# Three edits to the order of loads and turns in a graph network kernel: one load stage for attention tiles, an earlier transpose of f3, and a longer prefetch ahead of the expert weights

## The chip, the cores and the metric

The kernel runs on one core of a Trainium2 chip. The metric is the time of one execution on the device in microseconds (us), as a median over runs. The names of the engines: PE is TensorE (PEld its weight load), DVE is VectorE, ACT is ScalarE, POOL is GpSimd, SP is SyncE, which here only issues DMA transfers.

## The reference

The reference computes two layers of a graph network over 6250 nodes with 256 features and 100,000 edges, all in float32. Each layer has a message part over the edges, an attention part and a part with experts. Cut to the parts that the edits touch:

```python
# layer 0, attention: linear attention over all nodes, for each row n
q, k = elu(q) + 1, elu(k) + 1
kv = sum_n k[n] v[n]^T                      # per head
z  = 1 / (q . sum_n k[n] + 1e-6)
h  = x_norm + (q @ kv * z) @ w_out + b_out   # x_norm: layer norm of x
out = x + h * (1 + w_norm2 * rsqrt(mean(h * h) + 1e-6))

# layer 1: messages gathered over 100,000 edges, linear attention, sum into x3
f3 = layer_norm(x3)
# layer 1, experts: the router sees the mean of f3 and picks 2 of 8 experts for all rows
g  = softmax over the two picked router values
y  = sum_k g[k] * (gelu(f3 @ W1[k] + b1[k]) @ W2[k] + b2[k])
out = x3 + layer_norm(f3 + y) * gamma + beta
```

## The kernel before

The program is a sequence of phases. Inside a phase every engine has its own instruction stream, written out by the helper `timeline`: a plan gives each stage (a small function of a tile number i) the step at which it starts and a lag, and in each step an engine emits the stages that fall due in it, in the order of the plans. The streams of the engines share no clock. A stage waits on counting semaphores for what it needs (`Steps` for results, `Landing` for transfers), and every stream runs strictly in its own order. So a lag says where in the queue of its engine a stage stands, not when it runs.

Phase **g1** (about 60 to 980 us) is layer 0. POOL gathers rows of the normed input for 702 tiles of 128 edges, one indirect transfer per tile (line 891), in step k for tile k. PE multiplies each pair of gathered tiles with a one-hot matrix (`sums`, line 1285, ten steps after), and DVE adds the product into a ring (line 1098). Woven into that are the attention and the projection of the layer's first matrix (lines 1424 and 969). The attention runs over 50 tiles of 125 rows, one each seven steps (`ATT`), with four buffers (`AR = 4`). For tile i, SP loads `qt` (128 partitions, line 831), `xa` and `x0` (125 partitions each, lines 837 and 841). PE computes the denominators from `qt` eight steps after the tile's first step (line 1354); DVE adds the bias to `xa`, forms h (line 1174) and at the end adds `x0` to give "y" (line 1186, 29 or 30 steps after). Before the change `load_qt` and `load_xa` stand three steps ahead of the tile's first step and wait for "qz" and "h" of tile i-4; `load_x0` stands three steps after it and waits for "y" of tile i-4.

Phase **g2** (about 1680 to 2698 us) is layer 1's message part: 782 gathers (line 2516), two in each step; `sums` (line 2163) five steps after; the DVE add into the ring (line 2646) two steps after that. The PE stage `product(i)` (lines 2805 and 2810) makes the rows of x3 for tile i in step P9[i]+4; DVE's `x3_of(i)` follows in step P9[i]+5 (lines 2709 and 2711, then the row statistics). From step F3[i], which is 12 or more steps after P9[i]: `f3_of(i)` on DVE writes the normed tile (line 1489) in step F3[i], `turned(i)` on PE transposes it (line 2817) in F3[i]+3, `copy(i)` on ACT copies the result out of PSUM and sums it into `fsum` (line 2556) in F3[i]+4, and SP stores f3 (line 2503) in F3[i]+1 and the transposed tile (line 2507) in F3[i]+6. In a step, PE emits `sums` first, then the turns, then the product. `product(49)` is PE's last product; after it only turns are left.

Phase **p11** (from about 2699 us) is the expert part. DVE takes the mean of `fsum`, works out the router on one partition and writes `chosen`; SP reads the two expert numbers from it and loads the weights. Then 25 blocks of 250 rows run through a loop: `layer_up` (32 matmuls, line 2930), gelu on ACT (line 2968), `layer_down` (32 matmuls, line 2947), layer norm on DVE and POOL. PE runs `layer_up(0)`, then two small bias products (line 2939), then `layer_down(0)`, `layer_up(1)` and so on. The first `layer_up` waits for half k of `w1` at the matmuls that use it. SP's stream at the head of the phase: wait for all stores of g2, columns(0) (line 2874, f3 transposed, 128 partitions), rows(0) (lines 2878 and 2880, f3 and x3, 125 partitions), wait for `chosen`, w1 in two halves, b1 in two, columns(1), w2 and b2 in two halves each, gamma, beta, rows(1).

Of the kernel before, what the change touches and what calls it, by code (L numbers as in the profile page):

```python
# [31 lines left out]
N, D, E = 6250, 256, 100000  # L32
P = 128
TN = 125
BN = 2 * TN
NB = N // BN
DC = D // P
# [99 lines left out]
def gps_kernel(nc, A, out):  # L137
# [48 lines left out]
    def spread(dram):  # L186

        return dram.rearrange("(p t) f -> p t f", t=2 * NB)
# [4 lines left out]
    with top:  # L193
# [20 lines left out]
        s_w2 = sem("gin_w2")  # L214
# [410 lines left out]
        with Phase("g1") as ph:  # L625
# [109 lines left out]
            qt_in, xa_in, x0_in = (ph.landing(n, AR) for n in ("qt", "xa", "x0"))  # L735
# [29 lines left out]
            MIX = [QKV[-1] + 27]  # L765
# [33 lines left out]
            with nc.Block() as block:  # L799
                @block.sync  # L800
                def _(e):
# [25 lines left out]
                    def load_qt(i):  # L827
                        if i < 2:
                            q_out.wait(e, i, (NB - 1 - i) // 2)
                        zs.wait(e, i - AR, "qz")  # L830
                        qt_in.start(e.dma_start(qt[:, i % AR, :, :],
                                                q_d[i // 2].rearrange("p (c t n) -> p c t n", c=DC, t=2)
                                                [:, :, i % 2, :]), i % AR)

                    def load_xa(i):
                        hsum.wait(e, i - AR, "h")
                        xa_in.start(e.dma_start(xa[:, i % AR, :], spread(xn_d[0:N, :])[:, i, :]), i % AR)

                    def load_x0(i):
                        fin.wait(e, i - AR, "y")  # L840
                        x0_in.start(e.dma_start(x0[:, i % AR, :], spread(A["x"])[:, i, :]), i % AR)
# [31 lines left out]
                    def load_edges(i):  # L873
# [3 lines left out]
                             (QKV, [(load_xn, 0), (store_q, 23)]), (ATT, [(store_att, 33), (load_x0, 3), (load_xa, -3), (load_qt, -3)]),  # L877
# [115 lines left out]
                def _(e):  # L993
# [171 lines left out]
                    def add_xb(i):  # L1165
                        xa_in.wait(e, i % AR, i // AR)
                        hsum.done(e.tensor_tensor(xa[:, i % AR, :], xa[:, i % AR, :], bout[:, :], ALU.add), "xb")
# [13 lines left out]
                    def finish(i):  # L1181
                        gate.wait(e, i, "g")
                        fin.done(e.tensor_tensor(hh[:, i % AR, :], hh[:, i % AR, :], gw[:, :], ALU.mult), "gh")
                        fin.wait(e, i, "gh")
                        x0_in.wait(e, i % AR, i // AR)
                        fin.done(e.tensor_tensor(hh[:, i % AR, :], hh[:, i % AR, :], x0[:, i % AR, :], ALU.add), "y")
# [66 lines left out]
                def _(e):  # L1253
# [92 lines left out]
                    def denominators(i):  # L1346
                        qt_in.wait(e, i % AR, i // AR)
                        moved.wait(e, i - 1, "den")
                        if i <= ALONE:
                            hsum.wait(e, i - 1, "h")  # L1350
                        if i == 0:
                            mixed.wait(e, 0, "mix")
                        for c in range(DC):
                            mm = e.matmul(ps[:, 3, c * TN:(c + 1) * TN], ksd[:, c, :], qt[:, i % AR, c, :],
                                          start=True, stop=True)
                        dens.done(mm, "den")
# [978 lines left out]
        with Phase("g2") as ph:  # L2335
# [121 lines left out]
            with nc.Block() as block:  # L2457
                @block.sync
                def _(e):
# [45 lines left out]
                    def store_f3T(i):  # L2505
# [3 lines left out]
                             (P9, [(load, 0), (store_x3, 6)]), (F3, [(store_f3, 1), (store_f3T, 6)]))  # L2509
# [13 lines left out]
                def _(e):  # L2523
# [50 lines left out]
                    def do_silu(i):  # L2574
# [6 lines left out]
                             (KV, [(square, 5), (roots, 8)]), (PAIRS, [(deviations, 9)]), (F3, [(copy, 4)]))  # L2581
# [150 lines left out]
                def _(e):  # L2732
# [80 lines left out]
                    def turned(i):  # L2813
                        ln.norm.wait(e, i, "f")
                        copied.wait(e, i - 1, "c1")
                        for c in range(DC):
# [4 lines left out]
                             (KV, [(products, 11), (project, 3)]), (MIX, [(mix_wo, 1), (mix_wq, 3)]), (F3, [(turned, 3)]),  # L2821
# [3 lines left out]
        with Phase("p11") as ph:  # L2825
# [10 lines left out]
            s_in, s_b1, s_w2, s_sc, s_v, s_e, s_pe, s_sel = (  # L2836
                ph.sem(n) for n in ("in", "b1", "w2", "sc", "v", "e", "pe", "sel"))
            s_w1 = [ph.sem(f"w1_{k}") for k in range(2)]
# [26 lines left out]
            with nc.Block() as block:  # L2865
                @block.sync
                def _(e):
# [4 lines left out]
                    def load_columns(i, u, h):  # L2872
                        up.wait(e, i - 2, BANKS[-1])
                        c_in.start(e.dma_start(f3T[:, u, :, :], f3T_d[ds(i * 2, 2), :, :].rearrange("t p n -> p t n")), u)
# [10 lines left out]
                    load_columns(0, 0, 0)  # L2885
                    load_rows(0, 0, 0)
                    e.wait_ge(s_sel, 1)
                    x = [e.value_load(chosen[0:1, k:k + 1], min_val=0, max_val=NE1 - 1) for k in range(2)]  # L2888
                    for k in range(2):
                        e.dma_start(w1[:, k, :, :], A["L1_ffn_W1"][ds(x[k], 1), :, :]  # L2890
                                    .rearrange("e (c p) n -> p (e c) n", p=P)).then_inc(s_w1[k], 16)
# [3 lines left out]
                    load_columns(1, 1, 0)  # L2895
# [4 lines left out]
                    for to, src in ((gamma[:, :], A["L1_ffn_gamma"]), (beta[:, :], A["L1_ffn_beta"])):  # L2900
                        e.dma_start(to, src.partition_broadcast(TN)).then_inc(s_in, 16)
                    load_rows(1, 1, 0)
# [8 lines left out]
                def _(e):  # L2911
# [9 lines left out]
                    def layer_up(i, u, h):  # L2921
                        c_in.wait(e, u, h)
                        for q in range(FC):
                            act.wait(e, i - 1, BANKS[q])
                            for m in range(2):
                                k, f = divmod(2 * q + m, FC)
                                if isinstance(i, int) and i == 0 and f == 0:
                                    e.wait_ge(s_w1[k], 16)
# [161 lines left out]
```

## Time and profile before

| what | value |
|---|---|
| median of 3 runs | 3097.06 us (3095.69 to 3098.36) |
| the profiled execution | 3098.36 us, span of its trace 3096.8 us |
| PE busy | 2645.7 us, 85% of the span |
| DVE, ACT, POOL busy | 1716.6, 1447.5, 1817.0 us |
| granted clock of PE, mean | 0.945 of full speed |
| DMA | 464.78 MB, 150 GB/s over the span |

The span runs from the first to the last instruction of the trace. Busy shares are averages over phases with different limits, so they are read phase by phase. Times in the rows are microseconds from the start of the span. A row of a timeline has the start, the duration, the engine, the line of the kernel, the operation and its tensors (written tensor, then what it reads); "x8" means that many instructions in a row, and a bracket tells how long the engine sat idle before it and what ended that.

### The profile page before, as it was taken

To read this page: it belongs to the slowest core of one execution; us is meant where nothing else is said; L and a number is where in the kernel's file an instruction comes from. 1 tells how busy PE (TensorE), PEld (TensorE's weight loads), DVE (VectorE), ACT (ScalarE), POOL (GpSimd) and SP (SyncE) were. 2 spreads that over 40 slices of the span, in tenths; PEclk is the share of its full clock that TensorE was granted. 3 is DMA by queue.
4 is the path that set the end of the run, shared out by engine and by line. 5 is a ranking of instruction groups with operands and counts; after the bars stand their busy time and mean duration, and the time that the engine had idled before them with its cause. 6 is when DMAs were issued, how large, how long until landed. Compare 5 with 4: busy or idle time off the path is not lost. (4 is left out here: it accounts for less than half of the span.)

```text
span 3096.8 us, 54298 instructions
## 1 busy us (share of the span) xinstructions
PE 2645.7 (85%) x14909; PEld 2211.0 (71%) x14909; DVE 1716.6 (55%) x5340; ACT 1447.5 (47%) x4046; POOL 1817.0 (59%) x1962
## 2 busy tenths in 40 slices
PE   1999998999987997799932999999888888699998
PEld 1777777888886886688832676666677777578876
DVE  7733335787775667333355566566566767633333
ACT  4022222553322553233345988888566766422221
POOL 5777777777774355343376777777777777400000
PEclk9999999999998998899965999999899999899999
DMA  7364446777764674333367444444456665532221
GB/s 226 112 192 141 140 139 187 230 217 229 234 216 124 217 237 152 106 92 94 93 185 237 114 125 116 124 118 125 118 173 185 175 167 158 153 92 70 66 67 55
DMA packets 291701, 464.78 MB, mean 150 GB/s; under 512 B 91221, under 2 KB 224276, under 8 KB 290074
## 3 DMA queue, kind: packets, MB, share of 16 engines
q1 hardware_dynamic: 207804, 232.37, 25.4%
q0 software_dynamic: 81216, 221.98, 24.3%
q10 hardware_dynamic: 2402, 7.19, 0.7%
q8 instruction: 115, 1.88, 0.3%
q14 instruction: 164, 1.34, 0.1%
HBM read 349.16 MB, written 112.23 MB: 149 GB/s over the span
## 5 line engine op out<-in xcount | busy, mean ns | idle before, releaser
L2516 POOL DMA_INDIRECT g_got<-xm_d,idx x782 | 763.6, 977 | 252.9 <-issue 223.3
L891 POOL DMA_INDIRECT g_got<-xn_d,idx x702 | 682.0, 972 | 232.6 <-issue 212.4
L2163 PEld LDWEIGHTS ps<-g_hotw,g_got 128*128 128x128 f32 x3128 | 405.7, 197 | 207.9 <-DMA g_got<-xm_d,idx 107.2
L2163 PE MATMUL ps<-g_hotw,g_got 128*128 128x128 f32 (+11 forms) x3128 | 434.3, 288 | 128.8 <-DMA g_got<-xm_d,idx 70.9
L1285 PEld LDWEIGHTS ps<-g_hot,g_got 128*128 128x128 f32 x2808 | 354.5, 195 | 91.6 <-DMA g_got<-xn_d,idx 57.6
L1285 PE MATMUL ps<-g_hot,g_got 128*128 128x120 f32 (+4 forms) x2808 | 372.3, 280 | 44.5 <-DMA g_got<-xn_d,idx 41.7
L2565 ACT ACTIVATE g_hotw<-g_hot,g_wr 128x16 f32<-128x16 f32 (+8 forms) x1308 | 302.3, 308 | 125.7 <-DVE g_hot L598 125.0
L1485 POOL TENSOR_TENSOR p_ln_rs<-p_ln_pre,neg_half 125x2 f32<-125x2 f32 x50 | 35.2, 703 | 486.9 <-DVE p_ln_pre L1480 486.9
L2646 DVE TENSOR_TENSOR g_ring<-g_ring,ps 128x84 f32 (+10 forms) x391 | 133.4, 341 | 302.1 <-PE ps L2163 166.5
L2079 POOL DMA_INDIRECT z_d<-p_yj,p_to x108 | 121.9, 1128 | 204.8 <-DVE p_to L2112 182.9
L2968 ACT ACTIVATE p_hid<-ps,p_b 128x250 f32<-128x250 f32 x200 | 82.8, 465 | 279.4 <-PE ps L2930 279.4
L2043 PE MATMUL ps<-gin_hid,p_wj 128*128 128x256 f32 x864 | 198.1, 383 | 0.9 <-ACT gin_hid L1985 0.8
L2947 PE MATMUL ps<-p_w,p_hid 128*125 128x256 f32 x800 | 179.3, 382 | 22.1 <-ACT p_hid L2968 22.1
L1694 PE MATMUL ps<-gin_w,gin_hid 128*125 128x256 f32 x800 | 188.9, 386 | 9.1 <-POOL p_before L1753 9.1
L1424 PE MATMUL ps<-g_hT,g_w 128*128 128x250 f32 x800 | 190.4, 382 | 2.8 <-DVE g_hT L1110 2.8
L1098 DVE TENSOR_TENSOR g_ring<-g_ring,ps 128x40 f32 (+9 forms) x351 | 73.9, 211 | 203.8 <-PE ps L1285 122.9
L2947 PEld LDWEIGHTS ps<-p_w,p_hid 128*125 128x125 f32 x800 | 148.2, 188 | 52.9 <-ACT p_hid L2968 30.1
L2769 PE MATMUL ps<-g_half 128*125 128x512 f32 x400 | 185.8, 608 | 0.0
L2043 PEld LDWEIGHTS ps<-gin_hid,p_wj 128*128 128x128 f32 x864 | 165.7, 192 | 24.3 <-issue 1.1
L2930 PE MATMUL ps<-p_f3T,p_w 128*128 128x250 f32 x800 | 176.0, 377 | 3.7 <-DMA p_w<-in_L_ffn_W 3.7
L1994 ACT ACTIVATE gin_hid<-ps,p_wj 128x256 f32<-128x256 f32 x216 | 90.5, 470 | 189.3 <-PE ps L2043 189.3
L1694 PEld LDWEIGHTS ps<-gin_w,gin_hid 128*125 128x125 f32 x800 | 148.1, 190 | 30.0 <-issue 9.5
(376 smaller groups left out, 5026.9 us busy)
## 6 DMA issues: line engine op xcount, KB each, us to landing
h_d<-gin_hid SPq DMA_DIRECT2D x23, 1000.0 KB, 5.2
gin_hid<-h_d SPq DMA_DIRECT2D x23, 1000.0 KB
p_xr<-jobs_d SPq DMA_DIRECT2D x54, 258.0 KB, 2.7
g_got<-xm_d,idx POOLq DMA_INDIRECT x782
g_half<-xmT_d SPq DMA_DIRECT2D x100, 125.0 KB
g_got<-xn_d,idx POOLq DMA_INDIRECT x702
p_wj<-z_d SPq DMA_DIRECT2D x50, 224.0 KB
q_d<-g_qo SPq DMA_DIRECT2D x25, 250.0 KB
```

The lines of the kernel that those rows point to most:

```text
L891: landed.start(e.indirect_dma_start(got[:, k % (2 * GB), :], None, xn_d[0:N, :], bass.IndirectOffsetOnAxis(ap=idx[:, HT + k:HT + k + 1], a ...
L1285: mm = e.matmul(to, got[:, 2 * (g % GB) + j, c * P:(c + 1) * P], hot[:, g % HR, j, 0:w].unsqueeze(1).broadcast_to([P, r, w]), start=(j == ...
L1424: mm = e.matmul(ps[:, 5 + n % 2, k * BN:(k + 1) * BN], w1[:, c, f:f + P], hT[:, i % 2, c, :], start=(c == 0), stop=(c == DC - 1))
L1694: mm = e.matmul(ps[0:TN, i % 2, t * D:(t + 1) * D], hid[:, slot(i), c, t * TN:(t + 1) * TN], w2[:, c, :], start=(c == 0), stop=(c == HC - 1))
L2043: mm = e.matmul(ps[:, 2 * k + u, o * JOB:(o + 1) * JOB], w[:, c, o * P:(o + 1) * P], src[:, u, c, :], start=(c == 0), stop=(c == DC - 1))
L2163: mm = e.matmul(to, rows[j][:, c * P:(c + 1) * P], hotw[:, j, c * w:4 * w].unsqueeze(1).broadcast_to([P, r, n]), start=(j == 0), stop=(j = ...
L2516: landed.start(e.indirect_dma_start(got[:, 2 * (g % GB) + j, :], None, xm_d[0:N, :], bass.IndirectOffsetOnAxis(ap=idx[:, 2 * g + j:2 * g + ...
L2565: ins = e.activation(hotw[:, u, 1, m * w:(m + 1) * w], hot[:, u, 1, 0:w], ACT.Copy, scale=chunk(n)[:, k, m:m + 1])
L2646: added.done(e.tensor_tensor(to, to, sums_of(bank_of(g)[0], w, bank_of(g)[1]), ALU.add), "add")
L2769: mm = e.matmul(ps[0:TN, bank, :], kT[:, i % 2, c, :], wkv[:, c, at:at + INNER], start=(c == 0), stop=(c == DC - 1))
L2930: mm = e.matmul(ps[:, q, m * BN:(m + 1) * BN], w1[:, k, c, f * P:(f + 1) * P], f3T[:, u, :, c * TN:(c + 1) * TN], start=(c == 0), stop=(c ...
L2947: mm = e.matmul(ps[0:TN, 4 + u, t * D:(t + 1) * D], hid[:, u, k, f, t * TN:(t + 1) * TN], w2[:, k, f, :], start=(j == 0), stop=(j == 2 * F ...
```

## The change

Three edits, in three phases.

1. In g1 the three loads of an attention tile become one stage, `load_att`, in the tile's first step. All three wait for "y" of tile i-4 and count on one semaphore per buffer, which the three users wait for in full.
2. In g2 `turned`, `copy` and `store_f3T` each move two steps earlier: from F3+3, +4 and +6 to F3+1, +2 and +4.
3. In p11 the loads of columns(1), rows(1), gamma and beta move ahead of the wait for `chosen`, and so ahead of the weights; both halves of w1 count on one semaphore, and `layer_up(0)` waits for both at its start.

```diff
-            qt_in, xa_in, x0_in = (ph.landing(n, AR) for n in ("qt", "xa", "x0"))
+            a_in = ph.landing("a", AR, 3)
...
-                    def load_qt(i):
+                    def load_att(i):
                         if i < 2:
                             q_out.wait(e, i, (NB - 1 - i) // 2)
-                        zs.wait(e, i - AR, "qz")
-                        qt_in.start(e.dma_start(qt[:, i % AR, :, :],
-                                                q_d[i // 2].rearrange("p (c t n) -> p c t n", c=DC, t=2)
-                                                [:, :, i % 2, :]), i % AR)
-
-                    def load_xa(i):
-                        hsum.wait(e, i - AR, "h")
-                        xa_in.start(e.dma_start(xa[:, i % AR, :], spread(xn_d[0:N, :])[:, i, :]), i % AR)
-
-                    def load_x0(i):
                         fin.wait(e, i - AR, "y")
-                        x0_in.start(e.dma_start(x0[:, i % AR, :], spread(A["x"])[:, i, :]), i % AR)
+                        u = i % AR
+                        a_in.start(e.dma_start(qt[:, u, :, :],
+                                               q_d[i // 2].rearrange("p (c t n) -> p c t n", c=DC, t=2)
+                                               [:, :, i % 2, :]), u)
+                        a_in.start(e.dma_start(xa[:, u, :], spread(xn_d[0:N, :])[:, i, :]), u)
+                        a_in.start(e.dma_start(x0[:, u, :], spread(A["x"])[:, i, :]), u)
...
-                             (QKV, [(load_xn, 0), (store_q, 23)]), (ATT, [(store_att, 33), (load_x0, 3), (load_xa, -3), (load_qt, -3)]),
+                             (QKV, [(load_xn, 0), (store_q, 23)]), (ATT, [(store_att, 33), (load_att, 0)]),
...
-                             (P9, [(load, 0), (store_x3, 6)]), (F3, [(store_f3, 1), (store_f3T, 6)]))
+                             (P9, [(load, 0), (store_x3, 6)]), (F3, [(store_f3, 1), (store_f3T, 4)]))
...
-                             (KV, [(square, 5), (roots, 8)]), (PAIRS, [(deviations, 9)]), (F3, [(copy, 4)]))
+                             (KV, [(square, 5), (roots, 8)]), (PAIRS, [(deviations, 9)]), (F3, [(copy, 2)]))
...
-                             (KV, [(products, 11), (project, 3)]), (MIX, [(mix_wo, 1), (mix_wq, 3)]), (F3, [(turned, 3)]),
+                             (KV, [(products, 11), (project, 3)]), (MIX, [(mix_wo, 1), (mix_wq, 3)]), (F3, [(turned, 1)]),
...
-                    load_columns(0, 0, 0)
-                    load_rows(0, 0, 0)
+                    for i in range(2):
+                        load_columns(i, i, 0)
+                        load_rows(i, i, 0)
+                    for to, src in ((gamma[:, :], A["L1_ffn_gamma"]), (beta[:, :], A["L1_ffn_beta"])):
+                        e.dma_start(to, src.partition_broadcast(TN)).then_inc(s_in, 16)
                     e.wait_ge(s_sel, 1)
...
-                                    .rearrange("e (c p) n -> p (e c) n", p=P)).then_inc(s_w1[k], 16)
+                                    .rearrange("e (c p) n -> p (e c) n", p=P)).then_inc(s_w1, 16)
...
-                    load_columns(1, 1, 0)
...
-                    for to, src in ((gamma[:, :], A["L1_ffn_gamma"]), (beta[:, :], A["L1_ffn_beta"])):
-                        e.dma_start(to, src.partition_broadcast(TN)).then_inc(s_in, 16)
-                    load_rows(1, 1, 0)
...
                         c_in.wait(e, u, h)
+                        if isinstance(i, int) and i == 0:
+                            e.wait_ge(s_w1, 2 * 16)
...
-                                if isinstance(i, int) and i == 0 and f == 0:
-                                    e.wait_ge(s_w1[k], 16)
```

## Rows read from the trace of the kernel before

**Rows 1.** The page: POOL's busy tenths in 40 slices of the span.
```profile
POOL 5777777777774355343376777777777777400000
```

**Rows 2.** Windows of 40 us in g1, g2 and p11: engines' busy us, clock, DMA.
```profile
720.00:760.00 40.00, 36.55 (x239) 33.98 (x238) 31.44 (x88) 12.49 (x34) 30.25 (x33) 0.96 0.70 217
...
2600.00:2640.00 40.00, 32.27 (x205) 26.95 (x206) 28.41 (x84) 25.28 (x92) 30.25 (x33) 1.00 0.57 160
...
2900.00:2940.00 40.00, 37.30 (x172) 32.12 (x173) 12.24 (x30) 7.94 (x20) 1.38 (x2) 1.00 0.27 76
```

**Rows 3.** Who waited for whom from 600 to 960 us: total, times, longest.
```profile
PEld ps L1285 <- DMA g_got<-xn_d,idx: 18.7, 13, 3.9
...
POOL g_got L891 <- PE ps L1285: 10.7, 31, 1.6
```

**Rows 4.** Timeline in g1: the last addition, two loads, the denominators' matmuls.
```profile
765.49 0.42 DVE L1186 TENSOR_TENSOR g_hh<-g_hh,g_x 125x256 f32<-125x256 f32 x1
...
765.94 0.26 SPq L841 DMA_DIRECT2D g_x<-in_x  x1
...
766.64 0.53 SPq L831 DMA_DIRECT2D g_qt<-q_d  x1
...
770.76 0.62 PE L1354 MATMUL ps<-g_qt,g_ksd 128*128 128x125 f32 x4
```

**Rows 5.** DMA issues in g1: count, size, median us to landing.
```profile
h_d<-gin_hid SPq DMA_DIRECT2D x17, 1000.0 KB, 5.2
```

**Rows 6.** Timeline in g2: f3_of of one tile and the next x3_of.
```profile
2340.84 0.58 DVE L1489 TENSOR_SCALAR g_f<-g_half,g_ln_mv,g_ln_rs 125x256 f32<-125x256 f32 x1
...
2344.73 0.28 DVE L2709 SCALAR_TENSOR_TENSOR g_half<-ps,xm_mv,g_half 125x64 f32<-125x64 f32 x1
```

**Rows 7.** Timeline of g2's end: product(48), f3_of(45), x3_of(48), the last two turns.
```profile
2685.63 1.03 PE L2805 MATMUL ps<-g_mix,g_half 128*125 128x256 f32 x4
...
2686.49 1.64 PE L2810 MATMUL ps<-wm,g_ring 128*125 128x128 f32 x14
2686.71 0.41 DVE L1489 TENSOR_SCALAR g_f<-g_half,g_ln_mv,g_ln_rs 125x256 f32<-125x256 f32 x1
...
2688.17 0.28 DVE L2709 SCALAR_TENSOR_TENSOR g_half<-ps,xm_mv,g_half 125x64 f32<-125x64 f32 x1 [0.28 <-PE ps L2810]
...
2695.24 0.40 PE L2817 MATMUL ps<-ident,g_f 125*128 125x125 f32 x2 [0.80 <-ACT g_f3T L2556]
...
2696.44 0.47 PE L2817 MATMUL ps<-ident,g_f 125*128 125x125 f32 x2 [0.80 <-ACT g_f3T L2556]
```

**Rows 8.** The chain that ended last, at p11's head: start, duration, what.
```profile
2708.02 3.81 DMA p_w<-in_L_ffn_W
...
2711.96 9.56 PE ps L2930 x32
...
2722.57 7.12 PE ps L2947 x32
...
2732.59 14.10 issue
```

**Rows 9.** Timeline of SP at p11's head: x3(0), w1, x3(1).
```profile
2703.38 0.45 SPq L2880 DMA_DIRECT2D p_x<-x_d  x1
2708.02 1.32 SPq L2890 DMA_DIRECT2D p_w<-in_L_ffn_W  x2
...
2714.70 1.91 SPq L2880 DMA_DIRECT2D p_x<-x_d  x1
```

**Rows 10.** Windows at p11's head; the last three columns: clock, DMA share, GB/s.
```profile
2706.00:2708.00 2.00, 0.31 (x2) 0.31 (x2) 0.97 (x7) 0.20 (x1) 0.00 (x0) 0.50 0.34 120
...
2709.50:2712.00 2.50, 0.04 (x1) 0.07 (x1) 0.00 (x0) 0.00 (x0) 0.00 (x0) 0.50 0.97 354
...
2716.50:2719.00 2.50, 2.50 (x11) 2.15 (x11) 0.91 (x3) 2.16 (x5) 0.00 (x0) 0.87 0.30 68
2719.00:2722.00 3.00, 3.00 (x15) 2.37 (x15) 1.27 (x2) 1.27 (x4) 0.00 (x0) 1.00 0.34 120
```

More of the change, by code:

```diff
@@ L1165, in add_xb @@
                     def add_xb(i):
-                        xa_in.wait(e, i % AR, i // AR)
+                        a_in.wait(e, i % AR, i // AR)
                         hsum.done(e.tensor_tensor(xa[:, i % AR, :], xa[:, i % AR, :], bout[:, :], ALU.add), "xb")
@@ L1184, in finish @@
                         fin.wait(e, i, "gh")
-                        x0_in.wait(e, i % AR, i // AR)
                         fin.done(e.tensor_tensor(hh[:, i % AR, :], hh[:, i % AR, :], x0[:, i % AR, :], ALU.add), "y")
@@ L1346, in denominators @@
                     def denominators(i):
-                        qt_in.wait(e, i % AR, i // AR)
+                        a_in.wait(e, i % AR, i // AR)
                         moved.wait(e, i - 1, "den")
@@ L2835, in gps_kernel @@
             CAPACITY = -(-N * 5 // (4 * NE1))
-            s_in, s_b1, s_w2, s_sc, s_v, s_e, s_pe, s_sel = (
-                ph.sem(n) for n in ("in", "b1", "w2", "sc", "v", "e", "pe", "sel"))
-            s_w1 = [ph.sem(f"w1_{k}") for k in range(2)]
+            s_in, s_w1, s_b1, s_w2, s_sc, s_v, s_e, s_pe, s_sel = (
+                ph.sem(n) for n in ("in", "w1", "b1", "w2", "sc", "v", "e", "pe", "sel"))
             flat = wts[:, :, :].rearrange("p r k -> p (r k)")
```

## Prediction

> **What bounds the kernel now.** I read the page first, and there POOL's slices: a long row of 7s near the start is phase g1, a second one is g2, and the zeros at the end are the last phase, p11 [rows 1]. In the two plateaus the row gathers run. The windows say it in numbers: in g1 and in g2 POOL is busy 30.3 us of every 40 with 32 or 33 gathers, one per 1.25 us, whatever TensorE does; in p11 TensorE is busy 37 of 40 us and POOL 1.4 [rows 2]. From 600 to 960 us TensorE's weight load waits 18.7 us for gathered rows, POOL only 10.7 us for TensorE [rows 3]. So in g1 and g2 a short TensorE stall is made good unless it falls after the last gathers; in p11 anything that delays the first matmul moves the end by as much. There the chain runs from the first weight transfer (3.81 us) into TensorE, and then repeats one block each 14.8 us (the next pieces are 14.10 us of "issue" and 0.7 us of POOL) [rows 8].
>
> **Edit 1, the loads of the attention stage (`load_att`).** The same 150 loads are issued. qt and xa of tile i used to stand three steps earlier and to wait only for tile i-4's "qz" and "h"; now they wait, as x0 did, for tile i-4's last addition "y". What waits for them is `denominators(i)` on TensorE. The tightest place I found, by laying the additions against the matmuls: y ends at 765.91, SP issues 0.03 us later, and the matmul on qt of four tiles on starts at 770.76 [rows 4]: 4.8 us. Needed are three issues (two of them 0.26 and 0.53 us [rows 4], some 1.2 us together) and a landing. These loads show no landing time; the nearest row is the 1000 KB store with 5.2 us [rows 5], eight times the bytes. That bounds the shortfall at 1.2 + 5.2 - 4.8 = 1.6 us there; zero is the other end. Behind the waiting instruction on SP stand the 1000 KB stores and `load_own`, which already stood behind the same "y" through x0's wait. POOL's pace absorbs such a stall [rows 2, 3]. I take 0. Were the cover gone, the cost would be up to 1.6 us at each tight tile.
>
> **Edit 2, the f3 turn two steps earlier.** `turned(i)` on TensorE moves from three steps behind `f3_of(i)` on VectorE to one; copy and store follow. VectorE runs late against TensorE in g2, so TensorE will now stand until `f3_of` is done, and queued behind it is `product(j)`, which VectorE's x3 step awaits. Take the case at 2340: `f3_of` ends at 2341.42; a turn takes 0.4 us (2695.24) and a product 2.5 us (2685.63 to 2688.13) [rows 7], which gives 2344.4; x3 started at 2344.73 [rows 6]. So VectorE would just not wait: the stall eats TensorE's lead and no more. The same sum over the tiles 0 to 44, of which this row pair is one: where a product follows in the same step, the margin is between -0.2 and +2 us, so a few tenths may be lost at some, and POOL's pace covers them. One place is different: the last but one product. No gather is left to hide behind. `product(48)` started at 2685.63; now `turned(45)` stands ahead of it and waits for `f3_of(45)`, which ends at 2687.12. It then starts at 2687.12 + 0.05 + 0.4 = 2687.6, 2.0 us late, and x3(48) (2688.17 now), product(49) and the rest follow [rows 7]. Some is given back: today copy(46) is queued behind the last square root on ScalarE and delays three turns; in the new order it is done before. I take 0.5 us of a turn and copy's 1.2 us (two turns start at 2695.24 and 2696.44 [rows 7]), since the tail is then paced by `f3_of` instead. Net: +1.5 us at the end of g2's engines, between 0 (if VectorE's step comes earlier) and 2.0.
>
> **Edit 3, the head of p11.** Before, SP issued columns(0) and rows(0) (f3, x3), then waited for the router's choice and issued the weights. Now columns(1), rows(1), gamma and beta stand ahead of the weights. SP has the time: a load takes about 0.45 us to issue, the third ended at 2703.83, and w1 was issued at 2708.02 [rows 9]; six more end by 2706.5. But the transfers are not free. With rows(0) in flight the DMA engines move 120 GB/s at a share of 0.34, while the weights move 354 at 0.97 [rows 10]: a load over 125 rows keeps five or six of sixteen engines busy. And rows(0) ended only at about 2709.5, when w1 was ready to start. Everything put ahead of w1 on those few engines delays w1, since w1 needs all of them.
> The Trainium skill ("DMA: Bandwidth & Descriptors", Queues, rings and completion order; How many engines) states that a transfer is split over the largest k up to 16 that divides the slowest dimension (125 gives 5, 128 gives 16), on the lowest-numbered engines, each ring consumed in order. The share of 0.34 agrees with k = 5. By this rule the sum below holds; were all sixteen engines to share the load, it would be 2.9 us (the lower bound below).
> - f3(1) and x3(1): 250 KB each (256,000 bytes) at 120 GB/s: 2 x 2.13 = 4.3 us.
> - gamma and beta: 125 KB each at the same rate: 2 x 1.07 = 2.1 us.
> - columns(1): 250 KB over 128 rows, at 354 GB/s: 0.7 us.
>
> That is 7.1 us. Bounds: all 1,024,000 bytes at 354 GB/s would be 2.9 us; and one stretch of such loads, 2716.5 to 2719, moved only 68 GB/s [rows 10], 1.1 us lost, so up to 8.2. I take 7.1, since rows(0), the same kind of load in the same place, ran at 120.
> The first block now also waits for both halves of w1. Half a w1 is 524 KB; at 354 GB/s 1.5 us, against the issue distance of about 0.9 us between the two (two issues in 1.32 us [rows 9]). I take 1.4.
> Third, SP's first load waits for the landing of g2's stores. They come up to 1.5 us later by edit 2, but fewer are left in the queue; I take 0.8 (0 to 1.5).
> What no longer matters: w2 lands after w1, about 3 us of transfer later, while the first up-projection takes 9.56 us [rows 8]; VectorE's scaling of it (about 2.3 us) still fits. The router and the choice end before the queue is empty and are no longer the bound. SP may stall in issuing (x3(1) took 1.91 us to issue [rows 9]), yet it needs to have issued w1 only by about 2717.
> The clock: TensorE's first block began at a granted clock of 0.50; the mean of 2716.5 to 2719 is 0.87, then it is 1.00 [rows 10]. TensorE idles before as it does today, so I take the same. At best the half-speed stretch vanishes: a down-projection of 32 matmuls at full clock takes 7.12 us and this first up-projection 9.56 [rows 8], so the bound is -2.4 us.
>
> **Sum.** 7.1 + 1.4 + 0.8 = +9.3 us on a profiled execution of 3098.36 us (span 3096.8 and 1.56 around it): 3107.7. That execution is 1.3 us above the median of 3097.06; against the median the forecast is **3106.4 us**.
>
> **Rivals.** About 0.2% (6.2 us) is what a measurement of this kernel tells from no change.
> - *The weights are not held up behind the rows* (not slower). If w1's parts pass the queued rows, or the five engines are others each time, only the wait for both halves (1.4) and the end of g2 (1.5) remain: +2.9, 3100.0. For it: w1 never stood behind a queue in this trace. Against: after the weights, the rows issued meanwhile still move at 120 GB/s and 0.34 from 2719 to 2722 [rows 10], one after the other, not beside them. It decides if the loads ahead cost under 3.3 us together. Chance 0.10.
> - *The lost lead in g2 and g1 reaches the end* (slower still). TensorE now follows VectorE closely, so each late gather or dip of the clock can reach VectorE; and edit 1 adds stalls. Twenty tiles losing 0.2 to 0.3 us beyond what POOL covers give +5: 3111.5. Against: TensorE waits for gathers, and POOL does not wait [rows 3]. Chance 0.14.
> - *Edit 3's order is hidden and the new order helps* (faster). All loads but the weights are out of the way, the clock is up at once (-2.4), and g2's tail gains its 0.5 without the stall; with w1 as early as today that is 3094. It never gives over 0.2%; another 4 us would have to come from POOL's own waits (10.7 us for TensorE [rows 3]). Chance 0.04.
> - The forecast: 0.72.
>
> **How the numbers follow.** The forecast's own range is 3103 to 3110: 2.4 us off for the clock, 1 for the rows, on the other side 1 for the rows, 0.7 for the tail and 1.5 for stalls. The range reaches to the third case above and half-way to the first: 3101.5 to 3111.5; outside lie most of the first and the last rival. Slower by over 0.2%: forecast 0.72 less 0.05 for its low end, and 0.14, so 0.81. Within: 0.10 + 0.05 and most of the last rival, 0.16. Faster 0.03.
>
> **What would show it.** In the trace after: the DMA share near 0.34 and 120 GB/s from 2706 to about 2717; w1's landing about 2719 to 2721, 10 us after its issue; TensorE's first p11 matmul at about 2721 (2711.96 before); blocks 14.8 us apart after that. In g2: `turned` starting as `f3_of` ends, product(48) about 2 us later, last gather unmoved. In g1: few waits at the denominators, last gather unmoved. The prediction is wrong if w1 lands within 4 us of its issue, or if the last gathers have moved by over 1 us.

## The result, and the profile after

The changed kernel takes 3123.41 us (median of 6 runs, 3114.61 to 3129.86) against 3098.40 us for the kernel before in the same set (3095.69 to 3101.98). The ratio is 1.0078, with a 95% interval from 1.0061 to 1.0093: 24 us slower (19 to 29). The forecast was 3106.4 us, in a range up to 3111.5: the sign was right, the size far too small.

The two profiled executions, cut at the same events, tell where the time went (us; "g2's stretch" runs from the first gather's start to a point 1.0 us before the end of the last product's matmuls, the same in every trace, so only its differences are read; the next piece starts at the true end):

| piece | before | after | more |
|---|---|---|---|
| start to the first gather of g2 | 1679.8 | 1682.5 | +2.7 |
| g2's stretch | 1010.7 | 1024.6 | +13.9 |
| last product to SP's first load of p11 | 11.0 | 10.8 | -0.2 |
| SP's first load to TensorE's first p11 matmul ("the head") | 9.4 | 19.3 | +9.9 |
| from there to the end | 384.8 | 383.8 | -1.0 |

The +2.7 of the first piece says nothing: in the traces on the usual chips that lack edit 1 this piece ends between 1674.1 and 1685.8 us.

**The head.** Timeline of SP in the kernel after, as in [rows 9]; then the windows, as in [rows 10]; then the chain that ended last, as in [rows 8]:

```profile
2719.01 0.40 SPq L2867 DMA_DIRECT2D p_f3T<-f3T_d  x1
...
2721.40 2.64 SPq L2873 DMA_DIRECT2D p_x<-x_d  x1
2724.08 2.17 SPq L2882 DMA_DIRECT2D p_gamma<-in_L_ffn_gamma  x1
2726.29 0.95 SPq L2882 DMA_DIRECT2D p_beta<-in_L_ffn_beta  x1
2729.17 1.00 SPq L2886 DMA_DIRECT2D p_w<-in_L_ffn_W  x2
```

```profile
2724.00:2726.50 2.50, 0.58 (x2) 0.49 (x2) 0.62 (x5) 0.20 (x1) 0.00 (x0) 0.50 0.34 112
2726.50:2729.00 2.50, 0.00 (x0) 0.00 (x0) 0.00 (x0) 0.00 (x0) 0.00 (x0) 0.50 0.34 114
2729.00:2731.50 2.50, 0.00 (x0) 0.00 (x0) 0.00 (x0) 0.00 (x0) 0.00 (x0) 0.50 0.57 170
2731.50:2734.00 2.50, 0.00 (x0) 0.00 (x0) 0.00 (x0) 0.00 (x0) 0.00 (x0) 0.50 0.92 274
2734.00:2736.50 2.50, 0.00 (x0) 0.00 (x0) 0.00 (x0) 0.00 (x0) 0.00 (x0) 0.50 1.00 246
```

```profile
2729.78 8.44 DMA p_w<-in_L_ffn_W
2738.35 6.85 PE ps L2922 x24
```

The DMA share stands at 0.34 with 112 to 114 GB/s until the row loads are through, as forecast, and w1 takes 8.44 us from its issue (3.81 in [rows 8]). SP's issues stretch to 2.64 and 2.17 us, w1 is issued 10.2 us after SP's first load (5.5 before), and TensorE starts 19.3 us after that load. The late issue alone does not explain this: the share was still 0.34 when w1 went out.

**g2.** Who waited for whom from 2300 to 2620 us in the kernel after (total, times, longest):

```profile
PEld ps L2811 <- DVE g_f L1483: 46.2, 31, 3.2
PE ps L2811 <- DVE g_f L1483: 34.2, 26, 3.0
...
POOL g_got L2510 <- PE ps L2157: 11.0, 36, 0.3
PE ps L2157 <- DVE g_hot L598: 9.1, 7, 2.3
...
PE ps L2157 <- DVE g_ring L2640: 5.0, 4, 2.1
DVE g_half L2703 <- PE ps L2804: 4.1, 7, 1.6
```

The same view and stretch of the kernel before:

```profile
PE ps L2163 <- DVE g_hot L598: 24.2, 24, 3.5
...
PE ps L2163 <- DVE g_ring L2646: 12.1, 13, 1.8
...
PEld ps L2817 <- issue: 4.7, 14, 0.7
POOL g_got L2516 <- PE ps L2163: 4.6, 15, 0.3
...
DVE g_half L2709 <- PE ps L2810: 1.1, 2, 0.8
```

TensorE now stands 34 us at the turn, for `f3_of`; before, never. But it was not free before. At `sums` it stood 36.3 us for VectorE (24.2 and 12.1), against 14.1 us after. So here VectorE held TensorE already, and some 22 of the 34 us took the place of older waits. The view names the one-hot matrices (line 598) for most of them. The times of the instructions say otherwise: of the 126 `sums` that start here, 56 start 0.15 us after the end of the addition (line 2646) four groups back, which frees the PSUM bank that they write (the kernel has four in turn), while their own one-hot had been ready for some 5 us. In the kernel after it is 14 of 121. Over all 50 tiles 41 turns start within 0.2 us of the end of their `f3_of`, before none (0.5 us at the least). The gathers hardly move (POOL waits for TensorE 11.0 us instead of 4.6), but TensorE falls behind them. Windows of the stretch in which TensorE goes from `sums` 240 to 300, and from 300 to 390, before and then after (engines PE, PEld, DVE, ACT, POOL; clock, DMA share, GB/s):

```profile
2303.90:2466.50 162.60, 136.75 (x928) 117.14 (x927) 113.23 (x363) 115.90 (x401) 123.90 (x128) 0.96 0.65 186
...
2466.50:2684.40 217.90, 180.59 (x1183) 158.98 (x1183) 153.69 (x462) 133.44 (x503) 163.34 (x170) 0.95 0.59 164
```

```profile
2305.70:2477.80 172.10, 141.66 (x928) 124.25 (x928) 114.64 (x365) 114.55 (x405) 130.97 (x135) 0.91 0.65 182
...
2477.80:2696.90 219.10, 181.40 (x1182) 160.61 (x1182) 154.53 (x463) 133.91 (x499) 156.65 (x161) 0.94 0.57 159
```

The same 928 matmuls take 172.1 instead of 162.6 us: 4.9 more of busy time at a mean clock of 0.91 (0.96), and 4.6 more of idle time. (162.6 is the least of six traces with g2 as before, which take up to 171.0 us at clocks of 0.94 to 0.97. The lag at the last gather, below, tells the two kernels apart more clearly.) The gathers of 60 steps take 153.8 us, so even the kernel before falls back here: `sums` 300 starts 13.6 us after its gathers end, and 24.4 us after them in the kernel after. From 300 to 390 the gathers take 228 us and TensorE 218 to 219, so about 10 us are won back: 3.1 us are left at the last gather before (up to 8.7 in the other five of those traces, which win back 10 to 13 us), 13.6 after. What is beyond that reaches the end.

The order of the matmuls tells why this stretch. From `sums` 218 to 296 a product follows every three steps. With `turned` in F3+1 it falls into the same step as a product, ahead of it, at 30 places, 23 of them one after the other from 230 to 296; in F3+3 it does so at 2. At g2's end, where [rows 7] showed one late product, the chain goes hand to hand:

```profile
2699.88 0.41 DVE L1483 TENSOR_SCALAR g_f<-g_half,g_ln_mv,g_ln_rs 125x256 f32<-125x256 f32 x1
...
2700.34 0.55 PE L2811 MATMUL ps<-ident,g_f 125*128 125x125 f32 x2 [2.17 <-DVE g_f L1483]
...
2700.68 1.91 PE L2799 MATMUL ps<-g_mix,g_half 128*125 128x256 f32 x4
...
2702.39 2.39 PE L2804 MATMUL ps<-wm,g_ring 128*125 128x128 f32 x14
2704.82 0.28 DVE L2703 SCALAR_TENSOR_TENSOR g_half<-ps,xm_mv,g_half 125x64 f32<-125x64 f32 x1 [3.75 <-PE ps L2804]
```

**g1.** Waits from 600 to 960 us, as in [rows 3]:

```profile
POOL g_got L886 <- PE ps L1279: 10.0, 32, 0.5
...
PE ps L1348 <- DMA g_x<-in_x: 14.7, 12, 2.3
```

TensorE waits 12 times for the landing of an attention tile's loads, which it never did before; POOL's wait for TensorE stays at 10.0 us (10.7). The other kernels without edit 1 show 7.3 to 15.2 us here; those with it, e1 among them (15.7), 10.0 to 19.7.

### The profile page after: what moved, and what is told of

The parts are those of the page before. It is cut to its first block and busy times, and to the rows that moved or that the text cites. A ratio compares the mean times of both kernels' runs of the same rounds, so it can differ in the third digit from the quotient of the medians.

```text
span 3122.2 us, 54248 instructions
## 1 busy us (share of the span) xinstructions
PE 2645.5 (85%) x14909; PEld 2211.8 (71%) x14909; DVE 1716.8 (55%) x5340; ACT 1446.5 (46%) x4046; POOL 1819.7 (58%) x1962
## 5 line engine op out<-in xcount | busy, mean ns | idle before, releaser
L2157 PE MATMUL ps<-g_hotw,g_got 128*128 128x128 f32 (+11 forms) x3128 | 423.1, 285 | 95.9 <-DMA g_got<-xm_d,idx 66.6
L2922 PEld LDWEIGHTS ps<-p_f3T,p_w 128*128 128x128 f32 x800 | 151.3, 189 | 32.5 <-issue 12.9
```

Of the source, the lines that this page charges most:

```text
L2157: mm = e.matmul(to, rows[j][:, c * P:(c + 1) * P], hotw[:, j, c * w:4 * w].unsqueeze(1).broadcast_to([P, r, n]), start=(j == 0), stop=(j = ...
L2922: mm = e.matmul(ps[:, q, m * BN:(m + 1) * BN], w1[:, k, c, f * P:(f + 1) * P], f3T[:, u, :, c * TN:(c + 1) * TN], start=(c == 0), stop=(c ...
```

## The experiments

Ratios are against runs of the kernel before in the same set; the us beside them are the ratio times its median. Sets ran on different chips. On all but one the kernel before takes 3098 to 3101 us; in the set of e5 to e8 it takes 3527 us (last section), so there only ratios and the pieces of the trace are compared. Pieces, us, each from one profiled execution, which need not lie at the median (e2's is 7 us above its own, e15's 9 above, e11's 10 below):

| kernel | ratio (95%) | g2's stretch | head |
|---|---|---|---|
| before | 1 | 1010.7 | 9.4 |
| after | 1.0078 (1.0061 to 1.0093) | 1024.6 | 19.3 |
| e1, edit 1 | 1.0004 (0.9994 to 1.0014) | 1012.5 | 9.6 |
| e2, edit 2 | 1.0040 (1.0025 to 1.0056) | 1028.0 | 10.3 |
| e3, edit 3 | 1.0031 (1.0019 to 1.0043) | 1012.5 | 19.6 |
| e4, turn at F3+2 | 1.0011 (1.0000 to 1.0022) | 1017.7 | 10.5 |
| e9, e2 with product first | 1.0009 (0.9998 to 1.0020) | 1014.9 | 10.7 |
| e10, e3 with two waits | 1.0029 (1.0019 to 1.0039) | 1013.4 | 18.2 |
| e11, before, rows split | 1.0006 (0.9995 to 1.0017) | 1009.5 | 10.5 |
| e12, all edits mended | 1.0039 (1.0026 to 1.0053) | 1024.4 | 11.8 |
| e13, e2 with early f3_of | 1.0041 (1.0027 to 1.0055) | 1018.8 | 10.4 |
| e14, e12 with g2 as before | 1.0019 (1.0009 to 1.0029) | 1010.3 | 11.7 |
| e15, e12 with product first | 1.0025 (1.0014 to 1.0036) | 1018.2 | 11.8 |
| e16, before, product first | 1.0001 (0.9991 to 1.0010) | 1008.3 | 9.7 |
| e17, before, early f3_of | 1.0040 (1.0027 to 1.0054) | 1025.0 | 10.2 |
| e18, e13 with product first | 1.0025 (1.0015 to 1.0035) | 1015.5 | 9.8 |
| e5, turn alone (slow chip) | 1.0055 (1.0035 to 1.0074) | 1247.8 | 9.9 |
| e6, as e13 (slow chip) | 1.0017 (1.0004 to 1.0031) | 1230.1 | 10.5 |
| e7, columns(1) only (slow chip) | 1.0005 (0.9993 to 1.0018) | 1229.5 | 12.5 |
| e8, e3 with rows split (slow chip) | 1.0014 (1.0000 to 1.0028) | 1228.8 | 13.1 |

Six traces have g2 exactly as before (before, e1, e3, e10, e11, e14): 1009.5 to 1013.4 us. That spread of 4 us is the least that the rest of the column has to be held against: e12 and e13 have the same g2 and show 1024.4 and 1018.8.

**One edit at a time (e1, e2, e3).**

> Edit 1 alone (one load stage for qt, xa and x0). After the whole change the last gather of g1 ended 1.8 us later than before (962.2 against 960.4). Theory A (edit 1 makes the denominators wait for the loads and the slip reaches the end): the last gather of g1 about 1.8 us later and the time about +2, 3100. Theory B (the slip is chance, POOL's pace covers): last gather within 0.5 us of before and the time unchanged, 3098.

> Edit 2 alone (turned, copy and store two steps earlier). Theory A (TensorE, tied to VectorE's f3_of, loses its lead in the middle of g2 and cannot win it back before the gathers end): TensorE some 14 us behind the last gather instead of 3, so +12 to +16 us, about 3111; the groups 240 to 300 are where the lag builds. Theory B (the lead is lost only when edit 1 has shifted g1, or by chance of the clock): +1.5 us at the tail as predicted, 3099.5. Theory C (it is the earlier store on SP that holds back the loads of x3's tiles): same loss as A, but TensorE waits for those loads and not for f3_of.

> Edit 3 alone (six loads ahead of the weights, one wait for both halves of w1). Theory A (the head as the trace after shows it: 19.3 us from SP's first load to TensorE's first matmul, against 9.4 before): +9.9 us, 3108. Theory B (the head was long only because g2's tail came late): the predicted 7.1 + 1.4 = 8.5 or less.

The three sum to 0.4 + 4.0 + 3.1 = 7.5 thousandths, the whole change has 7.8: within their intervals the edits add up. Edit 2 gives +12.4 us by theory A, edit 3 +9.6 by theory A. C falls with e2's own waits: TensorE stands at the turn, for f3_of. Waits of e2 from 2300 to 2620:

```profile
PE ps L2817 <- DVE g_f L1489: 39.8, 27, 3.9
POOL g_got L2516 <- PE ps L2163: 15.4, 37, 2.4
```

Edit 1 is within what the runs tell from nothing (-2 to +4 us). The slip of g1's last gather (962.4) is no sign of it: e2 and e3, without edit 1, show 962.5 and 962.4.

**Half the way (e4), and the product first (e9, e16).** In e9 only TensorE's order in a step changes:

```diff
-                             ... (F3, [(turned, 1)]),
-                             (P9, [(product, 4)]))
+                             ... (P9, [(product, 4)]),
+                             (F3, [(turned, 1)]))
```

> Edit 2 by one step instead of two: turned in F3+2, copy in F3+3, store in F3+5. Theory A (the slack between VectorE and TensorE is what is lost, step by step): between before and e2_turn_only, some +2 to +6 us, with a few waits of TensorE for f3_of. Theory B (only the tightest lag couples the two engines): as before, within 1 us. Theory C (the store): half of e2_turn_only's loss.

> Edit 2 as it is, but within a step TensorE emits product(j) ahead of turned(i), so that the product is not queued behind the turn that waits for f3_of. Theory A1 (the loss goes through the product that stood behind the turn): most of the loss goes, under +4 us. Theory A2 (TensorE itself stands still, and the sums of the next steps are what comes late): most of it stays, +8 to +12, with TensorE still 25 us or more waiting for f3_of between g2's groups 240 and 360.

> The kernel before with product(j) ahead of turned(i) in TensorE's steps, the turn at F3+3 as it was. The turn has been ready for 2 us or more there, so nothing waits for it: theory A1 gives x3 its product 0.4 us earlier at 50 places and a time within 1 us of before, at best -1 to -2; a version that beats both kernels if anything here does.

e4 loses +3.4 us (0 to 6.8), as theory A has it. But its turns share a step with a product at 8 places only, none of them between `sums` 218 and 296, so it is also what the order of turn and product would give. e9 loses +2.8 (-0.6 to 6.2) instead of 12.4, though TensorE still stands for f3_of:

```profile
PE ps L2817 <- DVE g_f L1489: 23.1, 16, 4.2
```

That is A1's number: the loss goes when the product stands ahead of the turn. In part this is because the turn then comes later by the product's 2.5 us, which takes 17 us of the waits away; e9 does not separate the two. Who stands for the late product shows in the waits from 2300 to 2620 us, first of e2, then of e9:

```profile
ACT g_ring L2529 <- PE ps L2810: 61.9, 23, 4.3
...
DVE g_half L2709 <- PE ps L2810: 7.2, 6, 2.6
```

```profile
ACT g_ring L2529 <- PE ps L2810: 13.2, 8, 4.0
```

VectorE's x3_of waits 7.2 us for it in e2 (4.1 in the kernel after, 1.1 before) and never in e9. The longer wait is ScalarE's, which clears the piece of the ring that the product has read (line 2529): 61.9 us in e2, 57.0 in the kernel after, 13.1 in the kernel before and 13.2 in e9. It shows how late the products are, but only a little of a way back to TensorE: all idle times over 0.3 us before `sums` in this stretch of e2 end with an addition of VectorE, none with ScalarE's matrices, and TensorE's other waits for ScalarE grow from 3.1 us before to 6.6. e16 tests little: in the kernel before, turn and product share a step at 2 places, not at the 50 that its expectation took, so a time as before was all it could show.

**f3_of two steps earlier (e6, e13, e17, e18), the turn alone (e5).**

```diff
-                             (F3, [(f3_of, 0)]), (P9, [(x3_of, 5), (add_bias, 3)]))
+                             (F3, [(f3_of, -2)]), (P9, [(x3_of, 5), (add_bias, 3)]))
```

> Only TensorE's turn is moved (F3+3 to F3+1); ScalarE's copy stays at F3+4 and SP's store at F3+6. Measure in the trace: from g2's first gather to the end of its last product 1010.7 us before, 1028.0 in e2_turn_only. Theory A (TensorE standing at f3_of is the loss): the same 1022 to 1028 and about +12 us in time, 3112. Theory C (the early copy on ScalarE delays the scaled one-hot matrices, or the early store on SP the loads): this part alone stays near 1011 to 1014, time within 3 us of before.

> Edit 2 as it is, and VectorE's f3_of two steps earlier too (F3-2), so that three steps lie between f3_of and turned again. Theory A (the distance between f3_of and turned is what counts, not how early the turn is): TensorE's waits for f3_of, 40 us in 27 waits from 2300 to 2620 in e2_turn_only, fall below 5 us, the stretch is 1011 to 1014 us and the time within 3 us of before. Theory D (turns and copies that come early cost by themselves, by their place between the sums): loss stays near +12.

> The kernel of e6 again (edit 2 with f3_of two steps earlier), in the hope of a chip on which the gathers run at 1.25 us. g2's stretch from the first gather to the last product: 1009.5 to 1013.4 in the five traces with g2 as before, 1024.4 in e12 with f3_of earlier though TensorE waited for f3_of nowhere. Theory E1 (f3_of earlier brings back the distance and all of the loss): 1010 to 1015, time within 4 us of before; then e12's rest came from elsewhere. Theory E2 (early f3_of, turn and copy cost by themselves, as in D of e6): 1020 or more, +8 or more.

> The kernel before with one thing moved: VectorE's f3_of two steps earlier (F3-2); turn, copy and store where they were. Theory Q (f3_of's new place among VectorE's additions costs by itself; it explains e13's +12.7 without any wait of TensorE): +8 to +12, g2's stretch 1017 or more. Theory P (what costs in e13 is that turned(i) and product(j) stand in one step of TensorE, the turn first): no change, within 3 us of before, stretch 1009 to 1014.

> Edit 2 with both mends of g2: f3_of two steps earlier and product(j) ahead of turned(i). Theory P: as e9 or better, 0 to +4, stretch 1010 to 1015. Theory Q: as e13, +8 to +13.

e5 was a poor cut: with the copy left at F3+4, the turn of an odd tile now waits for the copy of the tile before, which ScalarE makes in that same step (25.7 us in 10 waits), so it brought a wait of its own, and its +19 us (12 to 26) don't tell what the turn alone costs. That the early copy and store cost little is shown by e9, which keeps both and loses +2.8. e6, on the same chip, had no more stretch than e7 and e8, and I took that for the proof that distance is all, though its time was +6.0 us (1.4 to 10.9). e13 refuted it: one turn of 50 starts within 0.2 us of f3_of, and still +12.7 us. e17 then puts the loss on f3_of's new place alone, +12.4 us with turn, copy and store untouched; e18, with the product first as well, is at +7.8, between the two theories. Windows from `sums` 240 to 300 of e17, then of e18:

```profile
2301.60:2474.90 173.30, 141.92 (x928) 120.92 (x927) 117.21 (x373) 116.16 (x401) 131.68 (x137) 0.94 0.66 183
```

```profile
2301.20:2467.40 166.20, 136.75 (x928) 118.03 (x928) 116.06 (x370) 115.02 (x405) 126.30 (x132) 0.96 0.67 186
```

e17 takes 173.3 us where the six traces with g2 as before take 162.6 to 171.0 (mean 166), without one wait of TensorE at the turn. The times show that f3_of must not come earlier in VectorE's queue, nor the turn ahead of the product in TensorE's: each engine's order is on the path. Where in g2 f3_of's new place costs is less clear: e13, with the same loss, takes 169.3 us in this stretch, inside the range of the six, and the idle times that end with VectorE's additions come to 48 us in e17 from 2300 to 2620 us, where the six show 37 to 50. No run isolates it.

**The head (e7, e8, e10, e11).** e8 and e11 split the row loads, e10 gives each half of w1 its own semaphore:

```diff
-                        f_in.start(e.dma_start(f3[:, u, :, :], rows_of(f3_d, i)), u)
+                        f_in.start_rows(e, f3[:, u, :, :], rows_of(f3_d, i), u)   # 112 and 13 rows
...
-                                    ...).then_inc(s_w1, 16)
+                                    ...).then_inc(s_w1[k], 16)
```

> Edit 3 cut down: only columns(1) goes ahead of the weights, with the one wait for both halves of w1; rows(1), gamma and beta stay behind the weights. From SP's first load of the expert phase to TensorE's first matmul: 9.4 us before, 19.6 in e3_head_only. Theory A (each load ahead costs its own transfer time, the four row loads most of it): 9.4 + 0.7 + 1.4 = 11.5, time +2, 3102. Theory B (the single wait for both halves, or the first extra load, makes most of it): 15 or more.

> Edit 3 as it is, but each load over 125 rows (f3, x3, gamma, beta) is made in two, 112 and 13 rows, so that it can spread over the DMA engines; twice as many issues. Theory A (the loads are slow because 125 rows keep five engines busy at 120 GB/s): the 1,024,000 bytes ahead move near 354 GB/s, 2.9 us, so the head takes 9.4 + 2.9 + 1.4, 13 to 15 us, and the time is about +4. Theory B (the cost is in SP's issuing, which stood 2.9 us at x3(1) and 2.2 us at gamma): it stays at 19 us or grows, +10.

> Edit 3 as it is, but each half of w1 counts on its own semaphore and TensorE waits for the second half only where it uses it, as before. Theory A (the joint wait is worth the time between the landings of the two halves): the head shortens from 19.6 to about 18.0 us, and the time is +8 instead of +10. Theory B (both halves land together behind the row loads, so the joint wait costs nothing): 19.3 to 19.7, unchanged.

> The kernel before, with nothing of the change, but each load over 125 rows in the expert phase made in two, 112 and 13 rows. Theory A (rows(0) was still moving when w1 was issued, on few engines): with rows(0) done earlier the head takes 8.5 to 9.2 us instead of 9.4 to 9.9; time -0.5 to -1, too little for the clock on the wall. Theory B (the choice of the experts alone sets w1's start, and its landing is its own 3.8 us): no change at all. g2 is untouched here, so its stretch is also the control of the other three.

e7: 12.5 us against 9.9 in e5, which has the head of before on that chip; 2.6 for columns(1) and the joint wait, forecast 2.1. e10: 18.2 against 19.6, so the joint wait is worth 1.5 us, forecast 1.4; its chain:

```profile
2710.27 7.92 DMA p_w<-in_L_ffn_W
...
2718.32 8.52 PE ps L2929 x32
```

e8: the same bytes as in e3, but 13.1 us, and the windows (first row columns(0), then the split rows) show why; below them the row loads of e3:

```profile
3124.30:3126.30 2.00, 0.00 (x0) 0.00 (x0) 1.41 (x9) 0.21 (x1) 0.00 (x0) 0.50 0.44 113
3126.30:3128.80 2.50, 0.00 (x0) 0.00 (x0) 2.05 (x14) 0.00 (x0) 0.00 (x0) 0.50 0.87 254
3128.80:3131.30 2.50, 0.58 (x2) 0.49 (x2) 0.90 (x6) 0.20 (x1) 0.00 (x0) 0.50 1.06 281
```

```profile
2714.00:2716.50 2.50, 0.46 (x2) 0.37 (x2) 0.16 (x1) 0.00 (x0) 0.00 (x0) 0.50 0.34 114
2716.50:2719.00 2.50, 0.00 (x0) 0.00 (x0) 0.00 (x0) 0.00 (x0) 0.00 (x0) 0.50 0.34 115
```

Twice the issues and 6.5 us less: not SP's issuing but the few engines under a load of 125 rows made the head long. By the rule of the Trainium skill, "DMA: Bandwidth & Descriptors" (Why a DMA increments its semaphore by 16 and not by 1, How many engines (k)), 125 rows come to 5 engines and 112 to 16; the shares of 0.34 and 0.87 to 1.06 agree. e11: in the kernel before, the same split wins nothing (10.5, where the traces with this head as before show 9.4 to 10.7): rows(0) is issued early, and the choice of the experts alone sets when w1 goes out, 6.5 us after SP's first load.

```profile
2695.47 0.41 SPq L2875 DMA_DIRECT2D p_f3T<-f3T_d  x1
...
2701.99 1.30 SPq L2891 DMA_DIRECT2D p_w<-in_L_ffn_W  x2
```

**All mended (e12, e14, e15).** Edits 1 and 3 with the rows split and two waits; g2 with early f3_of (e12), as before (e14), or with the product first (e15).

> The whole change with three mends: f3_of two steps earlier, the row loads of the expert phase in two parts, one semaphore for each half of w1. If the two causes found so far are all of the loss: g2's stretch as in the control of this set, the head 11 to 13 us, and the time +2 to +4 us instead of +24. If edit 1 costs too, or the edits add something together: +6 or more.

> e12 with g2 exactly as before: edit 1, and edit 3 with the rows split and a semaphore for each half. Theory E2 (e12's rest is g2's): head 11.5 to 12 us, g2's stretch 1010 to 1013, time +2 to +4. Theory E3 (e12's rest comes from edit 1 or from the edits together): +8 or more.

> e12 with another mend of g2: f3_of where it was, and product(j) ahead of turned(i) on TensorE. From e9 (+3 for edit 2 with the product first) and the head at 11.8 (+2): +5 to +6, g2's stretch 1013 to 1017. If e12's +12 comes from what both share (edit 1, the split rows, turns two steps early), it is +10 or more here too.

The heads are 11.7 to 11.8 us, 1 to 2 more than before. The rest of e12's +12.1 us is largely g2's: e14, which has g2 as before, loses 6 us less, and e13 and e17 lose 12 through g2 alone. e15 shows +7.8 and e14 +5.9 (2.8 to 9.0) where the head explains 1 to 2. The other 4 or so may be edit 1's; the intervals of e1 and e14 overlap, and they don't settle it. No version beats the kernel before; e16 and e11 equal it.

## Why the prediction was wrong

**The failed step is edit 2 in the middle of g2, put at 0 because "POOL's pace covers".** Worked from [rows 2, 3], that cover was a mean over g1 and the end of g2. In steps 218 to 296, with a tile every third step, TensorE is already slower than the gathers, and what holds it is VectorE, not POOL (36 us of waits for it from 2300 to 2620 us, a stretch for which the prediction read no waits). What it loses there it can win back only at about 10 us until the last gather, and the kernel before needs all of that. The stretch grew by 13.9 us in the whole change and 17.3 in e2, where I had 0 and 1.5 for the tail.

**Why the margins deceived me.** The margins of -0.2 to +2 us, taken one tile at a time from the trace before, held f3_of where TensorE's lead had let it be. But a late turn makes the product late, that x3_of, and that the next f3_of: a loop through two queues that can close every three steps (from 2300 to 2620 us VectorE waited for a product 7 times, before twice). e9 opens the loop and keeps over half of the waits, and most of the loss goes. That the loop back through x3_of is the reason fits the waits (4.1 us against 1.1), but they are short, e9 shortens TensorE's waits too, and no run tests it apart. The rival "lost lead" named this way with 0.14 and +5 us; its place was right, its size less than half.

**The tail of g2** was put at +1.5. In e9, with the same turns, `sums` 390 to the last product takes 7.2 us, as in the traces with g2 as before (6.1 to 7.7); in e2 it is 10.5 and in the kernel after 10.2 (all cut 1.0 us short, like the stretch). So +3, twice the size forecast. The order is the one forecast, but e17, whose turns are unmoved, has 10.2 too, and e12 and e13, with the same g2, 9.4 and 7.2; how much of the 3 is the turn's stays open.

**The head**, forecast +8.5 without the store term: +9.9 in the trace of the whole change, +10.2 in e3. The mechanism was right (few engines, in order, w1 behind them). Joint wait 1.4: 1.5 measured (e10). Rows, gamma, beta and columns(1) 7.1: 8.7 measured, the rest of e3's 10.2. (Heads that no edit touches vary from 9.4 to 10.7, so these are good to about 1 us.) The lower bound of 2.9 for all bytes on all engines: e8 gives 3.2 for it and the joint wait together. The rival "weights not held up" is out.

**The stores landing later**, +0.8: nothing; from the last product to SP's first load it is 10.8 us and was 11.0.

**The clock**: unchanged at the head (0.50), as taken; in g2 it was 0.91 in the stretch where TensorE now waits (0.94 to 0.97 with g2 as before), which the forecast had not. e12 shows 0.92 there without those waits, so they are not shown to be the cause.

**The signs named beforehand.** w1 did not land within 4 us of its issue (8.44). The last gathers did move by over 1 us (g1's by 1.8, g2's by 2.0), but so they do between traces with those phases unchanged, where g2's lies between 2667 and 2685 us: a sign too fine for single traces.

**Edit 1**, 0: waits at the denominators did come (12, up to 2.3 us, where "few" were forecast and 1.6 us was the bound), and POOL's waits did not grow in the kernel after (in e1 they were 15.7 us); the time, +1.2 (-1.9 to 4.3), doesn't contradict 0. That part of the cover argument, read from rows of the same phase, isn't refuted; e14's unexplained 4 us leave it open.

## What to carry to other kernels

Before work is called covered by another engine's pace, compare the two paces in the very stretch where the work falls, look at what the engine waits for there, and count how much lag can still be won back before the end; a mean over a phase hides the dense part. When a consumer moves closer to its producer on another engine, follow what is queued behind it around the loop back to the producer: margins read from the old trace don't hold once the loop closes. And loads put ahead of urgent ones are cheap only if their row count lets them spread over the DMA engines.

## What the runs showed of the hardware

One chip of those used runs this kernel 14% slower (3527 against 3100 us), at a mean TensorE clock of 0.90 instead of 0.945, and with gathers 1.54 us apart where the others do one in 1.28. Windows of 40 us in g2: first e7 on that chip, then the kernel before:

```profile
2100.00:2140.00 40.00, 31.44 (x145) 24.74 (x146) 17.72 (x61) 19.81 (x73) 24.27 (x25) 0.79 0.33 92
```

```profile
2100.00:2140.00 40.00, 36.27 (x200) 26.24 (x199) 25.16 (x74) 36.33 (x102) 30.56 (x32) 0.96 0.40 114
```

POOL issues 25 gathers instead of 32, and `sums` starts some 28 us after its gathers instead of 2 to 5, with 92 GB/s moved instead of 114. There the gathers' transfers seem to set the pace, but what slows them was not tried. The head is the same on both (9.9 and 10.5 us there, 9.4 to 10.7 elsewhere).

Single executions of the kernel before spread by 14 to 16 us within a set of 18 to 29 (22 us on the slow chip; 3089.67 to 3111.25 over the sets on the usual chips), so that no effect under some 3 us could be told from nothing.
